# Register waits in a gather, score and pool kernel: from instructions of their own to the instruction that follows

## The reference

```python
items_emb = item_table[items]
user_emb = user_table[users]
hist_emb = user_table[history_users]                      # 2048 x 100 x 128
scores = jnp.einsum('bhd,bd->bh', hist_emb, user_emb)
user_his_emb = jnp.einsum('bh,bhd->bd', scores, hist_emb)
x = jnp.concatenate([items_emb, user_his_emb, user_emb], axis=1)
x = _dice(_batchnorm(x @ W1 + b1, g1, be1), a1)           # 384 -> 1024
x = _dice(_batchnorm(x @ W2 + b2, g2, be2), a2)           # 1024 -> 512
return x @ W3 + b3
```

## Time and profile before

| | us |
|---|---|
| median of the runs (three, 1000.81 to 1003.52) | 1003.19 |
| the profiled execution, its own time | 1003.54 |
| its span, first to last instruction | 1001.5 |
| instructions counted in the page's first part (PE 3743, PEld 3743, DVE 1339, ACT 879, POOL 580) | 10284 in number |
| TensorE busy | 655.3 |
| VectorE busy | 520.6 |
| GpSimd busy | 490.8 |
| ScalarE busy | 338.9 |

### The profile page before, as it was taken

One profiled execution on the slowest core, in us unless ns is written; L12 is line 12 of the kernel. 1 busy time (PEld: TensorE's weight loads), 2 busy tenths in 40 slices (PEclk: granted clock), 3 DMA queues, 4 the chain that ended last, 5 costly groups with the idle time before them and its releaser, 6 DMA issues.

```text
span 1001.5 us, 16389 instructions
## 1 busy us (share of the span) xinstructions
PE 655.3 (65%) x3743; PEld 611.8 (61%) x3743; DVE 520.6 (52%) x1339; ACT 338.9 (34%) x879; POOL 490.8 (49%) x580
## 2 busy tenths in 40 slices
PE   4464655647474747466567465756766469999998
PEld 3463655547473736456467455755665469888888
DVE  7553444344453526354436354644344526999748
ACT  3111222223132313132223132332223237778546
POOL 6646544454555454636454635545544534281025
PEclk8776675757675666766676677858676679999999
DMA  7112111111111111111111111111111110000000
GB/s 218 38 35 44 35 34 35 35 42 33 42 36 39 30 45 26 44 27 42 32 38 33 45 25 42 35 34 39 40 34 33 43 22 1 2 0 1 1 1 2
DMA packets 17236, 34.61 MB, mean 35 GB/s; under 512 B 8104, under 2 KB 8400, under 8 KB 17168
## 3 DMA queue, kind: packets, MB, share of 16 engines
q0 software_dynamic: 14208, 29.13, 11.8%
q1 hardware_dynamic: 2960, 4.67, 1.4%
HBM read 33.76 MB, written 0.01 MB: 34 GB/s over the span
## 4 chain that ended last, share of the span: by engine, by line
PE 44%; another core or an unknown queue 26%; issue 15%; ACT 6%; DVE 4%; ACTq 4%; DVEq 1%; PEld 0%; PEldq 0%
PE ps L1489 14%; PE ps L1549 10%; PE ps L1409 7%; ACT scaled L1244 4%; PE ps L1425 3%; ACTq L1244 2%; PE ps L1475 2%; PE ps L1499 1%; PE ps L1564 1%; PE ps L1388 1%; ACT h L1230 1%; PE ps L1633 1%; PE ps L1430 1%; ACTq L1265 1%
## 5 line engine op out<-in xcount | busy, mean ns | idle before, releaser
L520 POOL DMA_INDIRECT rows<-in_L_rec_user_table_dram,slot_idx x432 | 411.6, 953 | 378.9 <-ACT scaled L1244 252.3
L1489 PE MATMUL ps<-ident,scaled 128*128 128x128 f32 x982 | 211.5, 384 | 228.1 <-ACT scaled L1244 188.0
L1489 PEld LDWEIGHTS ps<-ident,scaled 128*128 128x128 f32 x982 | 188.8, 285 | 245.6 <-issue 237.1
L1244 ACT ACTIVATE scaled<-rows,work 128x128 f32 (+1 forms) x491 | 157.3, 392 | 256.6 <-remote 162.0
L834 DVE TENSOR_TENSOR prod<-rows,ps 128x512 f32<-128x512 f32 x122 | 83.7, 686 | 152.9 <-issue 79.4
L711 DVE SCALAR_TENSOR_TENSOR h<-ps,col_no 128x1024 f32<-128x1024 f32 (+1 forms) x34 | 39.2, 1161 | 164.4 <-ACT ranked L1211 75.6
L1549 PE MATMUL ps<-h,w 128*128 128x256 f32 (+1 forms) x576 | 113.3, 356 | 1.0 <-DVE h L1064 1.0
L1409 PEld LDWEIGHTS ps<-wide,h 128*128 128x128 f32 x512 | 100.3, 297 | 16.9 <-issue 16.9
L1409 PE MATMUL ps<-wide,h 128*128 128x104 f32 x512 | 102.5, 382 | 9.7 <-issue 9.7
L1549 PEld LDWEIGHTS ps<-h,w 128*128 128x128 f32 x576 | 99.6, 190 | 12.8 <-issue 1.2
L840 DVE TENSOR_REDUCE work<-prod 128x512 f32 (+1 forms) x122 | 83.7, 686 | 35.3 <-issue 20.4
(11 more groups left out here) (219 smaller groups left out, 806.4 us busy)
## 6 DMA issues: line engine op xcount, KB each, us to landing
rows<-in_L_rec_user_table_dram,slot_idx POOLq DMA_INDIRECT x432
w<-in_L_rec_W_dram SPq DMA_DIRECT2D x1, 2048.0 KB
w<-in_L_rec_W_dram SPq DMA_DIRECT2D x1, 1536.0 KB
h<-in_r_history_users_dram SPq DMA_DIRECT2D x2, 400.0 KB, 3.5
wide<-in_L_rec_user_table_dram,own_idx POOLq DMA_INDIRECT x5
wide<-in_L_rec_item_table_dram,own_idx POOLq DMA_INDIRECT x5
last_row<-in_L_rec_user_table_dram SPq DMA_DIRECT2D x1, 64.0 KB
last_item<-in_L_rec_item_table_dram SPq DMA_DIRECT2D x1, 64.0 KB
```

The lines of the kernel that those rows point to most:

```text
L520: nc.gpsimd.indirect_dma_start(rows[:, s, :], None, user_table, bass.IndirectOffsetOnAxis(slot_idx[:, s:s + 1], 0)).then_inc(landed[s], 16)
L1244: nc.scalar.activation(scaled[:, j, :], rows[:, bass.ds((g & (GROUPS - 1)) * GROUP + j, 1), :], ACT.Copy, scale=score[:, bass.ds(g * GROUP ...
L1489: mm = nc.tensor.matmul(pooled_ps, scaled[:, j, :], ident[:, :], start=False, stop=False, skip_group_check=True)
```

## The change

`hold` no longer counts `passed`; the wait is then put on the instruction that follows. A new `hold_apart` does what `hold` did, and is called where the next operation is one of four kinds: the maximum and the replacement of the sorting, and the indirect DMAs of GpSimd. All other calls of `hold` stay as they stand.

```diff
         def hold(eng, semaphore, value):
+            if not isinstance(value, int) or value > 0:
+                eng.wait_ge(semaphore, value)
+
+        def hold_apart(eng, semaphore, value):
+            hold(eng, semaphore, value)
             if not isinstance(value, int):
-                eng.wait_ge(semaphore, value)
                 eng.sem_inc(passed, 1)
-            elif value > 0:
-                eng.wait_ge(semaphore, value)
...
-                    hold(pool, next_found[i], s + 1)
+                    hold_apart(pool, next_found[i], s + 1)
                     gather_own(i, next_row[:, i, :], next_idx[:, i:i + 1])
...
                     hold(pool, idx_ready, GROUPS * r + (q + 1))
-                    hold(pool, rows_free, GROUPS * r + (q - GROUPS + 1))
+                    hold_apart(pool, rows_free, GROUPS * r + (q - GROUPS + 1))
...
             def find_top(t, before):
-                hold(dve, keys_cut, before)
+                hold_apart(dve, keys_cut, before)
...
             def cut_top(t, before):
-                hold(dve, sorted_out, before + 1)
+                hold_apart(dve, sorted_out, before + 1)
```

## The result

The changed kernel took 995.54 us (median, 992.26 to 999.74) beside 1003.19 us before (1000.71 to 1006.80): a ratio of 0.9927, 95% interval 0.9898 to 0.9957. It is 7.65 us faster where 40 us were forecast. Inside the range, right in sign, wrong in size by a factor of five.

What follows compares the result with a forecast made beforehand. The stream was taken as bound by a pace of executed instructions, with 260 us of unexplained pauses. From 1003.54 us, 40 us for 1055 removed instructions and 0.35 us to the median came off: 963 us, range 942 to 1006.

Steps and rivals of the forecast that it cites:

- the second price: In the stream, a pace of executed instructions makes the pauses; 0.038 us an instruction, 40 us for 1055 removed.
- its own units: Stream's pace with an instruction weighing two and a gather packet one: 0.0190 us a unit, 0.038 us an instruction.
- Case (a): Likeliest rival: the stream's pace of instructions holds, 963 us, range 942 to 980; chance 0.5.
- What I took as a check: Dense layers' 14.4 counted instructions per us, without pause, were said to fit the stream's 17.3.
- The tiles' equal lengths: In the stream, two seven-group tiles took 44.0 and 43.8 us, eight-group ones 52.6: length follows the amount executed.
- The first price: In the stream, a wait moved off its instruction saves about 0.1 us a step; 10 to 37 us, 15 taken.
- case b: In the stream, only the step gets shorter and pauses have another cause: 988 us, 966 to 993; chance 0.25.
- (e): In the stream, shorter bursts make whole pauses vanish, 8 us a tile in 15 tiles: 883 us; chance 0.05.
- the gathers' 540 us a floor: GpSimd's 432 gathers at 1.25 us each set a 540 us floor under the stream, not reached.
- (d): Slower: register waits on TensorE's weight loads cost 0.14 us at 476 row additions, 67 us; 1030 us; chance 0.1.
- (c): No change: in the stream, the removed waits were hidden behind pauses of fixed length; 1003 us; chance 0.1.
- The count: Instructions expected gone: 494 on TensorE, 441 on VectorE, 120 on ScalarE, none on GpSimd; 1055 of 16389.

Runs made afterwards that it cites:

- all but VectorE merged: Changed kernel with all VectorE register waits on instructions of their own again, TensorE, ScalarE and GpSimd merged: 747.36 us, 0.9999 of the kernel before.
- the short matrices: Changed kernel, own rows' place matrix built for the first slot alone from the second tile on, output wrong: 745.79 us, 0.9964 of the kernel before.

## Why the prediction was wrong

- **The step that failed is the second price**, "If the stream runs at a pace of so many instructions per us, the price of one is the stream's time over its count", 0.038 us. The change removed 1163 instructions for 7.65 us, 0.0066 each. The stream's rate fell from 17.3 to 15.9 a us in the very measurement that the prediction was made for, and in its own units (an instruction two, a packet one) from 52.7 to 50.2; without pauses 9600 more instructions cost nothing. Case (a), which had a chance of 0.5, is out. The page of the Trainium skill that I weighed, "NOTIFIC — the notification-queue block", section 10 (an implicit record costs the engine nothing), agrees with the runs without pauses: 755.62 us with 9600 counts more, 757.49 without them. Its section 7.1 (the inner pipeline holds producers back) may still bear on the pauses; no run shows it.
- **What I took as a check was none.** A rate of 14.4 a us in the dense layers and 17.3 in the stream was called fitting; a stage bound by TensorE says nothing of a pace. Nor do the weights fit the two rates, as (a) has it: by them the stream makes 52.7 units a us and the dense layers 28.8 (2 x 2512 / 174.5). They were free choices, and they alone made 40 us out of 61. The tiles' equal lengths were picked too: all tiles of eight groups took 48.5 to 53.0 us, all of seven 41.3 to 46.1.
- **The first price was right in size**: 0.09 us a step was measured (0.27 to 0.18), and where the steps bound the stream the change gives 31.9 us, inside "10 to 37". With pauses I took 15 by that price (case b, 988 us, 966 to 993); 7.65 were had, just outside. Case (b)'s signs came, a rate that falls and pauses that keep their sum (88.0 and 86.3 us). What gave the 7.65 us is open: in the pair of profiles the difference lies in one pause of the last tile, which is the mechanism of (e) once and not fifteen times.
- **What bounds the stream.** The prediction called the gathers' 540 us a floor that is not reached. Without pauses it is reached and the other engines' work is hidden behind it, and the term that then decides is one I didn't have: where an operation of VectorE falls in a gather. I had said of VectorE's waits only what they save.
- **The rivals.** (d), slower through TensorE's weight loads, is refuted without pauses: 1.0005. Its sign did come there, but through VectorE. (c) is refuted by the interval.
- **The count** of 1055 missed GpSimd's 106 and two of ScalarE: in 104 of the 106 the wait for idx_ready went on the register arithmetic that lies between the two waits (78 times), or on the instruction that waits for rows_free (26 times). So an instruction can take two such waits, other than the section on the kernel before has it. The 7044 ns in GpSimd's row of line 394 are one of these 26, and have the second wait in them.
- **Not settled**: what the pauses of 8 us are. What is recorded with them: events lost, and register instructions of 0.7 us on VectorE, mostly while GpSimd's gathers kept 0.95 us and 0.30 between them (but between 54.7 and 61.6 us of the changed kernel's profile six of GpSimd's own took 0.49 to 0.73 us). They did not come back on the five chips, so nothing was tried on them.

Without pauses no kernel that computes the whole beats both: all but VectorE merged has 747.36 us, not to be told from before, and the short matrices leave out work.

## What to carry to other kernels

A large share of time that no wait explains must be seen in a second measurement of the same kernel before a forecast is built on it (here all seven runs of the first one had it, and none later); a mechanism fitted to one profile fits its accidents too. A wait made cheaper on an engine off the path still moves that engine's other work in time: where the bounding engine runs in a fixed rhythm and shares something with it, look which operation now starts where in that rhythm. A change of 0.1 us a step showed as 9 us (757.49 for 748.29) only through such a place.

## What the runs showed of the hardware

- A GpSimd gather of 128 rows takes 0.945 us and follows the last by 0.30. If it starts while VectorE runs lines 719 and 724 (1.03 us together, both inputs in SBUF), it ends 0.61 us after them, up to 1.58 us long in the changed kernel's profile; if it began before them, neither it nor they are longer. Between the kernels with full matrices the sum of the gathers goes from 411.0 to 420.6 us, 2.8 to 12.4 over 432 x 0.945.
- A register wait merged into the next instruction saves 0.09 us on VectorE (gap 0.27 to 0.18) and costs nothing measurable on TensorE's weight loads (1.0005 at 494 of them).
- 26027 instructions in a span of 753.2 us, 9600 of them counts on the otherwise idle SyncE, took no longer than 15226 (755.62 and 757.49 us).
- The same kernel, instruction for instruction, took 1003 us in the first measurement and 748 us on five chips afterwards; why is not known.
